# Layer norm rows moved from VectorE to ScalarE, with hand-written instruction orders rewritten in four places of each layer

## The chip, the cores and the metric

One Trainium2 chip, one core, no collectives. The metric is the device time in microseconds of one launch of the program (lower is better); every layer of every sequence runs inside that one launch.

## What is computed

Two sequences (BATCH = 2) of 1024 rows with 512 features go through two layers. A layer is attention followed by a small feed-forward product, each on a layer-normalised input and added to its input:

```python
x = x + attn(_layernorm(x), w_qkv, w_o)          # 32 heads of 16, 8 key/value heads, rope, causal softmax
x = x + scale * einsum(_layernorm(x), kernel*2-1) # kernel is 0/1, so the weights are -1/+1
```

`_layernorm` is `(x - mean) / sqrt(var + eps)` over the 512 features of a row, with no learned gain. The two layers differ in rope and in the layout of the weights. Everything is float32; the kernel keeps precision by splitting operands into a high and a low part and multiplying hi*hi + hi*lo + lo*hi.

## The kernel before, in words

A sequence is 8 tiles of 128 rows, kept in SBUF as `xs`. There are four rounds (2 sequences x 2 layers, `rounds`), written out one after the other, and each round has four stages. All five engines run their own program; nothing reorders it. The order on each engine is what the strings in the file say, and engines meet only through semaphores.

**Slots (first stage).** `SLOTS_A` counts slots n; `slot_work` turns a string of words into work, and `LAG` says for which tile t = n - lag a word works. In a slot TensorE turns one normalised tile (TX), multiplies the tile before by the qkv weights in four parts (Q.0 to Q.3), turns the head records of the tile two slots back in six quads (R.0 to R.5) into two PSUM banks, and computes row maxima products (U) of the tile three back. Behind Q stands a chain that crosses engines: ScalarE copies the projection (QC, `qkv_copy`), VectorE and GpSimd multiply by cos and sin (COS, `rope_sin`), VectorE adds (ROPE), ScalarE writes the high record parts (PH, `part_h`), GpSimd the low ones (`part_l`), and only then may R.0 of that tile start. The copies of R's quads are RC.1, 2, 4, 5 on ScalarE and RC.0, 3 on VectorE. The norm is made for a pair of tiles at a time: ST (`ln_stats`, VectorE), RS (`first_rstd`, ScalarE: Ln, then Exp), AP (`ln_a`, VectorE: four small Newton steps that refine 1/sqrt, and then two rows-times-scalar operations that write `xn`). HI and LO split a turned tile into its high part (ScalarE) and low part (VectorE).

**Groups 0 to 6.** For each of the 8 key/value heads, `GROUP_ORDER` interleaves on TensorE the softmax products S.p (two each, read by ScalarE's Exp at line 857), the value products PV, and the maxima products U.n of the *next* group, which VectorE reduces (`unit`, line 1027). The negated maxima are split by GpSimd (`nm_parts_of`), turned (N, `nm_turn`), copied to `nm_rows` by VectorE and sent by DMA (SP, line 463) to extra rows of `qT`, so that the product subtracts them. S.0 to S.4 need the maxima of chunk 0, S.5 and later those of chunk 1. X (`meet`) joins two halves of late maxima. The maxima of group 0 itself are made in the slots, those of the last tile (four units of 2 heads x 512 keys) after its last record copy and before S.0.

**Group 7 and the tail.** `LAST_ORDER` and `TAIL_ORDER` bring in, per tile, the turn and product of the output projection (CT, CP), its addition to `xs` (`add_wo`), the second norm (LS = `ln_stats`, LR = `first_rstd`, LM = `ln_newton`, LN = `ln_apply`, for tile pairs 0 to 3), the turn of the norm (DT, T), its split (H), the feed-forward product (DP) and its addition (`add_ffn`, line 1100). Pair 4 is pair 0 of the next round, and TA turns its first tile. WQ.c is ScalarE's split of a chunk of the next layer's qkv weights; GpSimd makes the low part of each chunk (line 1161, 128x768 with two SBUF inputs). DP of a tile waits for the addition of the tile two before it, since they share a PSUM bank.

In all orders an engine takes only its own words: of "T.4 DP.2 LM.3 WQ.0" TensorE takes T.4 and DP.2, VectorE the addition of DP.2 and then LM.3, ScalarE WQ.0.

## Time and profile before

| | us |
|---|---|
| device time, median of 3 runs | 1512.0 |
| the three runs | 1511.1, 1512.0, 1519.8 |
| the profiled execution's own time | 1511.48 |
| its span, first to last instruction | 1509.7 |
| TensorE busy | 1358.1 (90%) |
| VectorE busy | 1094.9 (73%) |
| ScalarE busy | 893.2 (59%) |
| GpSimd busy | 384.7 (25%) |

Times inside the trace are microseconds from the start of the span. A row of a timeline is: start, duration of the merged piece, engine, line, operation, output and input, how many instructions, and in brackets the idle time before it with what ended it.
### The profile page before, as it was taken

How to read it: one execution, taken by the hardware profiler on the slowest of the kernel's cores; microseconds unless marked ns; L12 is line 12 of the kernel's file. 1: busy time of each engine (PE TensorE's matmuls, PEld its weight loads, DVE VectorE, ACT ScalarE, POOL GpSimd, SP SyncE). 2: the span in 40 equal slices, each digit the busy share in tenths (PEclk: the TensorE clock that was granted, in tenths of full speed). 3: DMA queues.
4: the chain of work that ended last, by engine and by line, in shares of the span. 5: the costliest groups of instructions: out<-in, count | busy, mean ns of one | idle time of the engine just before them, and what ended most of it. 6: DMA issues, size and time to landing. Idle time of an engine off the chain costs nothing.

```text
span 1509.7 us, 28518 instructions
## 1 busy us (share of the span) xinstructions
PE 1358.1 (90%) x11076; PEld 796.5 (53%) x11076; DVE 1094.9 (73%) x1587; ACT 893.2 (59%) x1704; POOL 384.7 (25%) x591
## 2 busy tenths in 40 slices
PE   5989999999898999999889899999988889999997
PEld 4854444446675444444667544444567744444455
DVE  6667888847767888883776688888376668888647
ACT  3536776773354776775335377777624547777752
POOL 3422222111342222221134222222123412222201
PEclk9988999999897999999999699999999969999999
DMA  3000000001000000000220000000010000000011
GB/s 116 1 1 10 9 16 3 2 2 43 1 1 2 9 16 10 2 3 1 84 70 1 2 9 17 10 2 3 2 41 1 1 1 10 17 9 3 3 51 47
DMA packets 12980, 23.99 MB, mean 16 GB/s; under 512 B 1072, under 2 KB 4144, under 8 KB 12848
## 3 DMA queue, kind: packets, MB, share of 16 engines
q1 hardware_dynamic: 12848, 22.19, 4.3%
q8 instruction: 88, 1.44, 0.4%
q14 instruction: 44, 0.36, 0.1%
HBM read 16.94 MB, written 4.19 MB: 14 GB/s over the span
## 4 chain that ended last, share of the span: by engine, by line
PE 73%; DVE 16%; issue 6%; ACT 3%; POOL 1%; DMA 0%; DVEq 0%; ACTq 0%; POOLq 0%; SPq 0%
PE psO L675 20%; PE psM L539 15%; PE psE L654 14%; PE psM L612 12%; DVE mx L1027 8%; PE psE L592 3%; PE psO L592 3%; PE psM L522 2%; PE psM L619 2%; ACT probs L857 2%; DVE stats L934 1%; PE psM L639 1%; DVE xn L954 1%; DVE attn L1053 1%; PE psE L522 1%
## 5 line engine op out<-in xcount | busy, mean ns | idle before, releaser
L857 ACT ACTIVATE probs<-psE 128x512 f32<-128x512 f32 x1152 | 625.6, 596 | 293.4 <-PE psE L654 287.0
L1027 DVE TENSOR_REDUCE mx<-psM 128x2 f32<-128x768 f32 (+4 forms) x704 | 693.3, 1026 | 121.4 <-PE psM L619 96.3
L612 PE MATMUL psM<-kT,qT 48*128 48x384 f32 (+5 forms) x1536 | 314.5, 423 | 47.4 <-DVE mx L1027 36.6
L675 PE MATMUL psO<-probs,v_grp 128*32 128x512 f32 (+3 forms) x3072 | 324.3, 511 | 0.0
L654 PE MATMUL psE<-qT,kT 50*128 50x512 f32 (+3 forms) x1536 | 293.5, 420 | 15.3 <-ACT probs L857 10.2
L1227 POOL TENSOR_SCALAR_AFFINE_SELECT probs<-probs 128x512 f32<-128x512 f32 x256 | 160.0, 637 | 563.1 <-ACT probs L857 531.0
L612 PEld LDWEIGHTS psM<-kT,qT 48*128 48x128 f32 x1536 | 153.1, 196 | 161.6 <-DVE mx L1027 119.7
L654 PEld LDWEIGHTS psE<-qT,kT 50*128 50x128 f32 x1536 | 134.0, 191 | 171.6 <-ACT probs L857 127.2
L619 PE MATMUL psM<-mask_b 64*128 64x64 bf16 x2048 | 123.9, 201 | 0.0
L675 PEld LDWEIGHTS psO<-probs,v_grp 128*32 128x32 f32 x3072 | 68.4, 110 | 91.1 <-issue 68.5
L539 PE MATMUL psM<-wq_hi,xT_hi 128*128 128x512 f32 (+1 forms) x384 | 98.6, 379 | 9.2 <-ACT vs L823 4.7
L539 PE MATMUL psM<-w_lo,xT_hi 128*128 128x512 f32 (+1 forms) x384 | 96.2, 374 | 2.0 <-DVE w_lo L982 2.0
L539 PE MATMUL psM<-wq_hi,xT_lo 128*128 128x512 f32 (+1 forms) x384 | 93.3, 365 | 0.0
L619 PEld LDWEIGHTS psM<-mask_b 64*128 64x128 bf16 x2048 | 62.3, 100 | 57.6 <-issue 26.3
L809 ACT ACTIVATE xT_hi<-psM 128x512 fp32r<-128x512 f32 x64 | 37.7, 596 | 81.0 <-PE psM L522 66.5
L592 PE MATMUL psE<-ident,probs 128*128 128x128 f32 x384 | 66.8, 302 | 20.9 <-issue 15.0
L1174 POOL TENSOR_TENSOR attn<-attn,sin_s 128x320 f32<-128x320 f32 x64 | 64.5, 1028 | 50.5 <-ACT attn L822 50.0
L1183 POOL TENSOR_TENSOR probs<-attn,probs 128x512 fp32r<-128x512 f32 x32 | 41.9, 1308 | 137.7 <-ACT probs L834 137.7
L539 PEld LDWEIGHTS psM<-wq_hi,xT_hi 128*128 128x128 f32 x384 | 61.4, 190 | 22.3 <-issue 13.1
L539 PEld LDWEIGHTS psM<-w_lo,xT_hi 128*128 128x128 f32 x384 | 66.0, 195 | 12.8 <-DVE w_lo L982 2.7
L1001 DVE TENSOR_TENSOR attn<-attn,cos_s 128x640 f32<-128x640 f32 x32 | 32.2, 1005 | 54.8 <-ACT attn L822 54.0
L592 PEld LDWEIGHTS psE<-ident,probs 128*128 128x128 f32 x384 | 51.4, 155 | 36.6 <-issue 19.5
(80 smaller groups left out, 1304.0 us busy)
## 6 DMA issues: line engine op xcount, KB each, us to landing
probs<-in_w_qkv SPq DMA_DIRECT2D x5, 1536.0 KB, 6.5
xs<-in_x SPq DMA_DIRECT2D x8, 512.0 KB, 3.8
xn<-in_w_o SPq DMA_DIRECT2D x16, 256.0 KB, 2.5
out_x<-xs SPq DMA_DIRECT2D x8, 512.0 KB, 2.8
qT<-nm_rows SPq DMA_DIRECT2D x128, 8.0 KB
probs<-in_w_ffn SPq DMA_DIRECT2D x1, 256.0 KB, 8.3
attn<-in_mask SPq DMA_DIRECT2D x1, 160.0 KB, 7.8
sin_s<-in_sin SPq DMA_DIRECT2D x1, 128.0 KB, 8.0
```

Of the source, the lines that this page charges most:

```text
L522: ins = pe.transpose(dst[:, c * P:(c + 1) * P], src[:, c * P:(c + 1) * P], ident[:])
L539: ins = pe.matmul(dst, xT[:, k, c, :], w[:, c, n0:n1], start=first and i == 0, stop=last and i == len(some) - 1)
L592: ins = pe.transpose(bank[:, n * P:(n + 1) * P], src, ident[:])
L612: return pe.matmul(psM[:, 2 * pair + h % 2, to:to + k1 - k0], qT[lo:lo + MAXROW, g, qt // QT_PER_CHUNK, h // 2, qt % QT_PER_CHUNK * P:(qt ...
L619: return pe.matmul(psM[:, 2 * pair + h % 2, k0:k0 + P // 2], late_b[lo:lo + ROW, half, :], half_b[lo:lo + ROW, :], start=False, stop=half ...
L654: ins = pe.matmul(psE[:, (2 * p + a) % SRING, to:to + w], kT[lo:lo + DEPTH, g, kb * P:(kb + 1) * P], qT[lo:lo + DEPTH, g, c, j // 2, off:o ...
L675: ins = pe.matmul(psO[VW * j:VW * (j + 1), off:off + w], v_grp[:, kb, :], probs[:, (g * NS + s) % PSLOTS, at(j), to:to + w], start=s in (0 ...
L857: act.activation(probs[:, (g * NS + s) % PSLOTS, at(heads[0]):at(heads[0]) + len(heads), 0:w], psE[:, n % SRING, 0:w * len(heads)].rearran ...
L1027: dve.tensor_reduce(to, src, AX.X, ALU.max, negate=True).then_inc(ring_used.sem, 1)
L1174: ins = pool.tensor_tensor(t4[:, :, a, :], x4[:, :, 1 - a, :], sn[:, :, a * HALF:(a + 1) * HALF].to_broadcast([P, HEADS + KV, HALF]), ALU. ...
L1183: pool.tensor_tensor(q_parts[:, t % RECS, :, 2, :], rq, q_parts[:, t % RECS, :, 0, :].bitcast(F32), ALU.subtract)
L1227: ins = pool.affine_select(out=d, in_=d, compare_op=ALU.is_ge, fill=0.0, base=0, pattern=[[0, REP], [1, P]], channel_multiplier=-1)
```

## The change

Four things are changed; no matmul is added or removed.

1. **Norm.** ScalarE writes `xn` as mean - x (Identity, scale -1, bias from `mv`), with no rstd in it, right after the statistics. The Newton steps stay on VectorE (NW in slots, LM in the tail) with their sign turned, so that the two signs cancel. rstd is applied after the product: by ScalarE in the three copies of `qkv_copy`, as a per-row scale, and by VectorE in `add_ffn`, where the scalar is now rstd * scale. Statistics of a pair now wait until ScalarE has read those of two pairs before.
2. **First slots.** In slot 2 TensorE does the whole of Q of tile 2 before R of tile 0, and ScalarE's QC comes before RC. ST, RS and the norm stand in later slots (the next round's pair 1 is measured at the very end of the tail, LS.5).
3. **Last slots and group 0.** N of chunk 0 stands behind R.1 in the last slot. The last tile's four maxima units leave the slots and become V.0 to V.3 in `FIRST_ORDER`, an order of group 0's own; Y is their `meet`, and chunk 1's N and GpSimd's split of it come inside group 0.
4. **Group 7 and the tail.** New `LAST_ORDER` and `TAIL_ORDER`: DT.0 goes ahead of S.16, T.6 ahead of DP.4, T.7 ahead of DP.5, WQ.0 to WQ.3 earlier, and the norm's steps are spread anew.

```diff
@@ orders @@
+FIRST_ORDER = """
+V.0 S.0 V.1 S.1 V.2 S.2 V.3 Y S.3 U.0 PV.0.0 S.4 U.1 PV.1.0 N.1.0 U.2 PV.2.0 OC.0.0 U.3
+S.5 U.4 O.0.0 S.6 U.5 S.7 U.6 U.7 S.8 U.8 PV.3.0 S.9 U.9 U.10 S.10 PV.4.0 U.11 S.11 U.12 S.12 U.13 PV.5.0
...
-S.14 CP.2 LR.0 LM.0 LN.0 S.15 PV.6.0 CP.3 LS.1
-S.16 DT.0 S.17 PV.7.0 DT.1 LR.1 LM.1 LN.1 PV.8.0 PV.9.0
+S.14 CP.2 S.15 PV.6.0 DT.0 LR.0 S.16 CP.3 S.17 PV.7.0 DT.1 LS.1 LM.0 PV.8.0 PV.9.0
...
-CP.7 H.3 LS.3 LR.3 T.4 DP.2 LM.3 WQ.0 T.5 H.4 LN.3 WQ.1 DP.3 H.5 WQ.2 LS.4 DP.4 T.6 H.6 LR.4 WQ.3 DP.5
-LM.4 T.7 LN.4 H.7 DP.6 TA.0 DP.7
+DP.0 LN.1 LR.1 O.1.0 DP.1 LM.1 CT.4 CT.5 CP.4 CT.6 CP.5 CT.7 LS.2 T.2 CP.6 T.3 H.2 LN.2 LR.2 LM.2
+CP.7 H.3 LS.3 T.4 WQ.0 DP.2 WQ.1 H.4 T.5 LN.3 DP.3 LR.3 H.5 T.6 LS.4 WQ.2 DP.4 WQ.3 H.6 T.7 LN.4 LR.4 LM.3
+DP.5 H.7 DP.6 TA.0 LM.4 DP.7 LS.5
...
-       "RC": 2, "ST": -4, "RS": -3, "AP": -2}
-PE_SLOT = "TX U.0 Q.0 R.0 R.1 U.1 Q.1 R.2 U.2 R.3 Q.2 R.4 U.3 R.5 Q.3"
-ACT_SLOT = "HI RC.1 RC.2 RS PH RC.4 RC.5 QC"
-DVE_SLOT = "AP COS U.0 RC.0 LO ROPE U.1 RC.3 U.2 ST U.3"
-SLOTS_A = range(-4, TILES + 4)
-SLOT_NM = TILES + 1
+       "RC": 2, "ST": -3, "RS": -2, "NW": -1, "AP": -2}
+SLOT_FILL, SLOT_LAST = 2, TILES + 1
+PE_SLOT = {None: "TX U.0 Q.0 R.0 R.1 U.1 Q.1 R.2 U.2 R.3 Q.2 R.4 U.3 R.5 Q.3"}
+ACT_SLOT = {None: "HI AP RC.1 RC.2 RS PH RC.4 RC.5 QC"}
+DVE_SLOT = {None: "COS U.0 RC.0 LO ROPE U.1 RC.3 U.2 NW ST U.3"}
+PE_SLOT[SLOT_FILL] = "TX Q.0 Q.1 Q.2 Q.3 R.0 R.1 R.2 R.3 R.4 R.5"
+ACT_SLOT[SLOT_FILL] = "HI AP RS QC RC.1 RC.2 PH RC.4 RC.5"
+DVE_SLOT[SLOT_FILL] = "COS LO ROPE RC.0 RC.3 NW ST"
+PE_SLOT[SLOT_LAST] = "U.0 U.1 R.0 R.1 N U.2 R.2 R.3 U.3 R.4 R.5"
+DVE_SLOT[SLOT_LAST] = "U.0 U.1 RC.0 N U.2 RC.3 U.3"
+SLOTS_A = range(-4, TILES + 2)
@@ ScalarE @@
+            def ln_apply(q, i):
+
+                act.wait_ge(var_ready.sem, var_ready.after(q))
+                for k in range(2):
+                    act.activation(xn[:, k, :], tile_of(i % PAIRS, k), ACT.Identity, bias=mv[:, i % 2, k, 0:1],
+                                   scale=-1.0).then_inc(xn_ready.sem, 1)
...
+                def ln_d(i):
+
+                    if i == 0:
+                        act.wait_ge(ring_ready.sem, ring_ready.after(r * NJ + JOB["O", KV - 1, 0]))
+                    last = TILES - 1 if i == 0 else d_turn(2 * i - 1)
+                    act.wait_ge(turned.sem, turned.after(r * TURNS + last))
+                    ln_apply(r * (2 * PAIRS) + PAIRS + i, i)
...
                 def qkv_copy(t, k):
+                    if t % 2 == 0:
+                        act.wait_ge(lm_self.sem, lm_self.after((r * (2 * PAIRS) + t // 2) * LM_LINKS + 3))
                     act.wait_ge(projected.sem, projected.after(r * TURNS + t))
                     bank = qkv_bank(t)
-                    act.activation(qk[:, k, 0:DIM], psM[:, bank, :], ACT.Copy)
+                    by = rstd[:, t // 2, k:k + 1]
+                    act.activation(qk[:, k, 0:DIM], psM[:, bank, :], ACT.Copy, scale=by)
...
@@ VectorE @@
+                if q >= 2:
+                    wait_alone(dve, xn_ready.sem, xn_ready.after(q * 2 - 3))
+                    wait_alone(dve, rs_ready.sem, rs_ready.after(q - 2))
...
-                link(lm_self, q * LM_LINKS + 2, dve.tensor_scalar(newton[:], newton2[:], -0.5, 1.5, ALU.mult, ALU.add))
-                dve.tensor_tensor(rstd[:, i % 2], y, newton[:], ALU.mult).then_inc(lm_self.sem, 1)
-
-            def ln_apply(q, i):
-
-                wait_alone(dve, lm_self.sem, lm_self.after(q * LM_LINKS + 3))
-                for k in range(2):
-                    dve.tensor_scalar(xn[:, k, :], tile_of(i % PAIRS, k), mv[:, i % 2, k, 0:1], rstd[:, i % 2, k:k + 1],
-                                      ALU.subtract, ALU.mult).then_inc(xn_ready.sem, 1)
+                link(lm_self, q * LM_LINKS + 2, dve.tensor_scalar(newton[:, i % 2], newton2[:, i % 2], 0.5, 1.5, ALU.mult, ALU.subtract))
+                if to is None:
+                    dve.tensor_tensor(rstd[:, at], y, newton[:, i % 2], ALU.mult).then_inc(lm_self.sem, 1)
...
                 def add_ffn(t):
-                    dve.wait_ge(projected.sem, projected.after(r * TURNS + d_turn(t)))
-                    dve.scalar_tensor_tensor(out=xs[:, t, :], in0=psM[:, 2 + t % 2, :], scalar=scale_s[:, 0:1],
+                    if t % 2 == 0:
+                        dve.wait_ge(lm_self.sem, lm_self.after((r * (2 * PAIRS) + PAIRS + t // 2) * LM_LINKS + 3))
+                    wait_alone(dve, projected.sem, projected.after(r * TURNS + d_turn(t)))
+                    dve.scalar_tensor_tensor(out=xs[:, t, :], in0=psM[:, 2 + t % 2, :], scalar=rstd[:, PAIRS + t // 2, t % 2:t % 2 + 1],
                                              in1=xs[:, t, :], op0=ALU.mult, op1=ALU.add).then_inc(ffn_added.sem, 1)
...
@@ GpSimd @@
                         mask(g, s)
+                        if g == 0 and s == DIAGONAL[1]:
+                            nm_parts_of(0, 1)
...
                 nm_parts_of(0, 0)
-                nm_parts_of(0, 1)
                 group(0, True)
```

TensorE in slot 2 of a round: L522 (L546 after the change) turns a normalised tile, L539 (L563) is Q, L592 (L616) is R. Before:

```order
L522 MATMUL psE<-ident,xn 128x128 x4
L539 MATMUL psM<-wq_hi,xT_hi 128x512 x4
L592 MATMUL psE<-ident,probs 128x128 x4
L592 MATMUL psO<-ident,probs 128x128 x4
L539 MATMUL psM<-w_lo,xT_hi 128x512 x4
L592 MATMUL psE<-ident,probs 128x128 x4
```

The same slot after the change:

```order
L546 MATMUL psE<-ident,xn 128x128 x4
L563 MATMUL psM<-wq_hi,xT_hi 128x512 x4
L563 MATMUL psM<-w_lo,xT_hi 128x512 x4
L563 MATMUL psM<-wq_hi,xT_lo 128x512 x4
L563 MATMUL psM<-wq_hi,xT_hi 128x256 x4
L563 MATMUL psM<-w_lo,xT_hi 128x256 x4
L563 MATMUL psM<-wq_hi,xT_lo 128x256 x4
L616 MATMUL psE<-ident,probs 128x128 x4
L616 MATMUL psO<-ident,probs 128x128 x4
```

Six parts of Q stood around and behind the first R; now all of them stand ahead of it, and the six R follow one another.

TensorE from the last slots into group 0: L639 (L663) is N, L612 (L636) and L619 (L643) a maxima product and its mask, L654 (L678) an S. Before, from the end of the slot that has N behind it:

```order
L592 MATMUL psO<-ident,probs 128x128 x4
L639 MATMUL psE<-ident,nm_parts 128x128
L612 MATMUL psM<-kT,qT 128x448 x2
L592 MATMUL psE<-ident,probs 128x128 x4
```

```order
L592 MATMUL psO<-ident,probs 128x128 x4
L612 MATMUL psM<-kT,qT 128x512 x4
L619 MATMUL psM<-mask_b 128x64 x4
L612 MATMUL psM<-kT,qT 128x512 x4
L619 MATMUL psM<-mask_b 128x64 x4
L654 MATMUL psE<-qT,kT 128x512 x2
```

And after the change, the same two places:

```order
L616 MATMUL psO<-ident,probs 128x128 x4
L636 MATMUL psM<-kT,qT 128x448 x4
L643 MATMUL psM<-mask_b 128x64 x4
L616 MATMUL psE<-ident,probs 128x128 x4
L616 MATMUL psO<-ident,probs 128x128 x4
L663 MATMUL psE<-ident,nm_parts 128x128
```

```order
L616 MATMUL psO<-ident,probs 128x128 x4
L636 MATMUL psM<-kT,qT 128x512 x2
L678 MATMUL psE<-qT,kT 128x512 x2
L636 MATMUL psM<-kT,qT 128x512 x2
L643 MATMUL psM<-mask_b 128x64 x4
L678 MATMUL psE<-qT,kT 128x512 x2
L636 MATMUL psM<-kT,qT 128x512 x2
```

Two maxima products and two R now stand ahead of N, and an S stands between the last tile's maxima products.

VectorE in the tail: L973 (L1016) is the low part of a turned tile, L945 to L948 (L997 to L1003) the Newton steps, L954 the norm's rows, L1100 (L1147) the feed-forward addition, L934 to L939 the statistics. Before:

```order
L939 TENSOR_SCALAR var_eps<-mv 128x2
L1100 SCALAR_TENSOR_TENSOR xs<-psM,scale_s,xs 128x512
L945 TENSOR_TENSOR newton<-rs0 128x2
L946 TENSOR_TENSOR newton2<-newton,var_eps 128x2
L947 TENSOR_SCALAR newton<-newton2 128x2
L948 TENSOR_TENSOR rstd<-rs0,newton 128x2
L973 TENSOR_TENSOR xT_lo<-psM,xT_hi 128x512
L954 TENSOR_SCALAR xn<-xs,mv,rstd 128x512 x2
L1100 SCALAR_TENSOR_TENSOR xs<-psM,scale_s,xs 128x512
L973 TENSOR_TENSOR xT_lo<-psM,xT_hi 128x512
```

After, from the statistics of the same pair (pair 3) on:

```order
L991 TENSOR_SCALAR var_eps<-mv 128x2
L1147 SCALAR_TENSOR_TENSOR xs<-psM,rstd,xs 128x512
L1016 TENSOR_TENSOR xT_lo<-psM,xT_hi 128x512
L1147 SCALAR_TENSOR_TENSOR xs<-psM,rstd,xs 128x512
L1016 TENSOR_TENSOR xT_lo<-psM,xT_hi 128x512
L986 BN_STATS stats<-xs 128x6 x2
```

Between the first addition and the low part that the next product waits for, four Newton steps are gone; the rows of the norm are gone from this engine, and the Newton steps of the pair come two statistics later.

## Rows read from the trace of the kernel before

**Rows 1.** The page, busy time and granted clock in 40 slices.
```profile
PE 1358.1 (90%) x11076; PEld 796.5 (53%) x11076; DVE 1094.9 (73%) x1587; ACT 893.2 (59%) x1704; POOL 384.7 (25%) x591
...
PEclk9988999999897999999999699999999969999999
```

**Rows 2.** The waits: engine and line, releaser, us in total, times, longest.
```profile
PE psE L592 <- issue: 15.0, 4, 3.8
...
PE psM L539 <- DVE xT_lo L973: 12.7, 4, 4.5
...
PE psE L639 <- POOL nm_parts L1217: 9.6, 4, 2.4
...
PE psE L522 <- DVE xn L954: 18.9, 8, 9.5
```

**Rows 3.** Windows: us, then busy PE, PEld, DVE, ACT, POOL, then PEclk, DMA.
```profile
475.30:511.20 35.90, 32.37 (x278) 16.05 (x278) 28.38 (x33) 20.04 (x38) 6.08 (x13) 0.81 0.03 9
511.20:539.10 27.90, 26.33 (x272) 12.38 (x270) 23.56 (x29) 20.90 (x40) 7.33 (x14) 1.00 0.04 12
460.10:475.30 15.20, 11.88 (x81) 8.30 (x81) 11.32 (x15) 6.04 (x10) 4.47 (x6) 0.89 0.01 3
745.00:763.00 18.00, 11.66 (x50) 8.86 (x51) 16.21 (x25) 4.81 (x9) 8.29 (x6) 0.91 0.33 118
763.00:787.20 24.20, 20.17 (x121) 17.52 (x120) 15.96 (x38) 10.87 (x25) 8.30 (x9) 0.86 0.14 44
```

**Rows 4.** Timeline of TensorE in the second round's tail.
```profile
748.92 2.07 PE L539 MATMUL psM<-wf_s,xT_lo 128*128 128x512 f32 x4 [2.72 <-DVE xT_lo L973]
...
759.91 0.66 PE L522 MATMUL psE<-ident,xn 128*128 128x128 f32 x4 [2.88 <-DVE xn L954]
```

**Rows 5.** Timeline of VectorE in the same tail.
```profile
744.90 1.61 DVE L947 TENSOR_SCALAR newton<-newton 128x2 f32<-128x2 f32 x1
746.65 1.61 DVE L948 TENSOR_TENSOR rstd<-rs,newton 128x2 f32<-128x2 f32 x1
748.18 0.68 DVE L973 TENSOR_TENSOR xT_lo<-psM,xT_hi 128x512 fp32r<-128x512 f32 x1
```

**Rows 6.** Timeline of GpSimd in the same tail.
```profile
744.64 5.38 POOL L1161 TENSOR_TENSOR w_lo<-probs,wq_hi 128x768 fp32r<-128x768 f32 x3 [30.12 <-ACT wq_hi L802]
```

**Rows 7.** Groups by line and form: count, busy us, mean ns of one, idle before.
```profile
L954 DVE TENSOR_SCALAR xn<-xs,mv,rstd 128x512 f32<-128x512 f32 x66 | 39.0, 632 | 12.9 <-PE psE L522 8.8 <-DVE rstd L948 4.0
...
L809 ACT ACTIVATE xT_hi<-psM 128x512 fp32r<-128x512 f32 x64 | 37.7, 596 | 81.0 <-PE psM L522 66.5 <-PE psM L539 14.5
...
L792 ACT ACTIVATE ln_var<-mv,eps_s 128x2 f32<-128x2 f32 x33 | 9.7, 295 | 46.9 <-DVE mv L937 46.9
...
L794 ACT ACTIVATE rs<-ln_var 128x2 f32<-128x2 f32 x33 | 6.7, 203 | 1.0
```

**Rows 8.** Timeline of TensorE, first slots of the third round.
```profile
762.61 1.18 PE L539 MATMUL psM<-wq_hi,xT_hi 128*128 128x512 f32 x4
...
772.28 1.17 PE L539 MATMUL psM<-wq_hi,xT_hi 128*128 128x512 f32 x4
777.17 1.08 PE L592 MATMUL psE<-ident,probs 128*128 128x128 f32 x4 [3.72 <-issue]
...
785.69 0.60 PE L522 MATMUL psE<-ident,xn 128*128 128x128 f32 x4
```

**Rows 9.** Timelines of VectorE, ScalarE and GpSimd in the same slots.
```profile
770.36 0.83 DVE L1001 TENSOR_TENSOR attn<-attn,cos_s 128x640 f32<-128x640 f32 x1 [0.22 <-DVE var_eps L939]
...
772.61 1.06 ACT L833 ACTIVATE probs<-attn 128x1024 fp32r<-128x1024 f32 x1 [2.23 <-DVE attn L1009]
...
774.37 1.43 POOL L1183 TENSOR_TENSOR probs<-attn,probs 128x512 fp32r<-128x512 f32 x1 [4.54 <-ACT probs L834]
```

**Rows 10.** Timeline of TensorE, the second round's first S.
```profile
478.73 0.70 PE L654 MATMUL psE<-qT,kT 50*128 50x512 f32 x2
```

**Rows 11.** Timeline of SyncE's DMA issues after chunk 1's maxima copy.
```profile
484.26 1.26 SPq L463 DMA_DIRECT2D qT<-nm_rows  x2
```

124 lines of the change are left out of this document (69 added, 55 removed).

## The prediction

> **What bounds the kernel now.** I read the page first. TensorE is busy 90% of the span, no other engine over 73%, and its granted clock dips at the same places of all four rounds [rows 1]. So time can come only from TensorE's idle stretches and from the stretches at the lower of its two clock levels that follow them; nothing in the change shortens a matmul. Next the waits: one gap of 3.7 to 3.8 us before the record turns (L592), one of up to 4.5 us before the low products (L539), one of 2.4 us before the turn of the maxima (L639) occur four times each, once per round; the wait of the norm's turn for VectorE's rows (18.9 us in 8 places, of which 9.5 is the start of the program) is the fourth [rows 2]. Then windows around these places in one round of about 371 us [rows 3]. The steady groups are nearly full (TensorE 26.33 of 27.90 us at clock 1.00) and the change leaves groups 1 to 6 alone. What can be gained lies in four stretches, and I price each from there.
>
> **The tail.** In 745 to 763 TensorE is idle 18.00 - 11.66 = 6.3 us [rows 3]. The timeline shows why: the product of tile 4 waits 2.72 us for its low part, the turn of the next round's first tile 2.88 us for its rows [rows 4]. VectorE does that low part at 748.18, behind two Newton steps of 1.61 us each [rows 5]; the same four-step group has 128x2 operands and costs about 0.3 us a step elsewhere. GpSimd runs three 128x768 differences from 744.64, 5.38/3 = 1.8 us each [rows 6], and both steps end as one of these ends. So VectorE is both the bottleneck here (busy 16.2 of 18 us) and held up by GpSimd. 
> After the change: the two norm-row operations per pair leave VectorE (66 in all, mean 632 ns, [rows 7]: 1.3 us a pair), and Newton leaves the path from statistics to turn. The new path is statistics (2 x 0.64 + 0.5 us), then ScalarE's rows. ScalarE's copy of 128x512 takes 596 ns; the per-row operand costs what L792 (with one) has over L794 (without), 295 - 203 = 92 ns [rows 7], so 0.69 us a row tile. For pair 3 I follow the new orders: product of tile 7 ends 740.2, statistics to 743.1, rows by 744.4, and TensorE reaches T.6 at 744.9. No wait. The low part of tile 4 is then delayed only by var_eps waiting for GpSimd (up to 1.6 us): at 746.3 instead of 748.9, about 0.5 to 1 us of idle. DP.6 and DP.7 wait for additions two tiles back, another 1 us in all. So the next Q starts near 756 and not at 762.6. The 6.3 us idle plus about 1.2 us of halved clock (2.07 us for four matmuls that take 1.08 at full clock, [rows 4]) is 7.5; I keep 1.5 of it: gain 6.0 us, bounds 2 (another small VectorE step behind each of GpSimd's four) and 7.5.
>
> **First slots.** From the first Q at 762.61 to the turn that opens slot 3 at 785.69 are 23.1 us [rows 8]. Q with its turn takes (772.28 - 762.61)/2 = 4.8 us. The third Q is begun at 772.28 and its rest stands behind R.0, which waits 3.72 us and then runs with everything else at half clock: clock 0.86 over 24.2 us means 6.8 us at the lower level, some 2.5 us lost [rows 3, 8]. R.0's own chain is Q.3, QC, sin and cos, add, high part (1.6 us), low part (1.43 us and more) [rows 9]; cos began at 770.36 because statistics stood before it on VectorE. Those are gone from there; cos starts when QC ends, and R.0 is ready about 1.5 us sooner. The three pointer scales in QC put 0.28 us back. After: three Q back to back, 3 x 4.7 = 14.1 us, by when R.0 is ready (14.5 before, about 13.3 now). Then six R over two banks, each pair of R held by one copy of 0.6 to 0.7 us and its turn of 0.6: about 4.0 us where they were hidden before. Then PH of tile 1 stands behind RC.2 and R.0 of tile 1 comes 1 us late in slot 3. 14.1 + 4.0 + 1.0 = 19.1: gain 4.0. Bounds 0 (clock falls again in the sparse R stage, and lateness grows) and 6.2.
> The norm's ScalarE rows in slots 0, 2, 4 (1.3 us each) fill ScalarE's idle time: it is busy 10.87 of 24.2 us [rows 3]. I cost them at nothing; if the cover fails, 1.3 us three times a round.
>
> **Last slot.** N waits 2.4 us for GpSimd [rows 2]; the four matmul groups behind it run at half clock (0.89 over 15.2 us is 3.3 us at the lower level, some 1.5 us lost, [rows 3]). Now two maxima products (1.2 us) go first and R.0 waits for the same GpSimd work minus its last 0.6 us. 2.4 + 1.5 - 0.9 = 3.0 us. Bounds 1 and 4.
>
> **Group 0.** From the last tile's maxima to the next group's first S are 35.9 us, with VectorE busy 28.38 and TensorE 32.37 at clock 0.81 [rows 3]; before the first S at 478.73 [rows 10] TensorE waits three times for VectorE's maxima. All that VectorE work stays, in a single mixed stretch. A steady group has VectorE idle for 27.90 - 23.56 = 4.3 us. TensorE at full clock needs about the 26.3 us of a steady group. So VectorE sets the length: 28.4 + 4.3 = 32.7. A new wait: chunk 1's maxima go meet, GpSimd, N, copy, two DMA issues (1.26 us, [rows 11]), flight, S.5, with only U.2, PV.2 and U.3 between N and S.5. No row shows the flight; bounded by 0 and by the distance from issue to the S.5 that used it before, about 6 us. I take 2 us, near the 2.5 of the w_o loads, and then S.5 waits 1 to 2 us, half of it inside VectorE's 4.3. 35.9 - 32.7 = 3.2, less 0.4 more idle: about 3.0. Bounds -2 and 5.
>
> **Group 7** and the part of the tail before 745 have TensorE over 97% full, so T.6, T.7 and DT.0 earlier bring nothing beyond the tail term. At the start of the program the weights' low parts are the limit: 0.
>
> **Sum.** 6.0 + 4.0 + 3.0 + 3.0 = 16.0 us a round, 64 us in four. The profiled execution took 1511.5 (span 1509.7 and 1.8 around it), 0.5 under the median, which is nothing here. 1511.5 - 64 = 1447.5, on the median's scale 1448. The bounds add to 1 and 22.7 a round, that is 1508 and 1421; not all fall on one side together.
>
> **Rivals.**
> (a) Only the tail and the last slot pay; group 0 takes the rest back as VectorE's 28.4 us plus S.5's wait, and the R stage pulls the clock down. 6 + 3 = 9 less 1 a round: 36 - 4 = 32 us, 1480. For it: VectorE stands at 28.38 of 35.9 there already, and the R stage is sparse. Against: the low clock of that window (0.81) has idle time as its cause, and this is what goes.
> (b) All gaps close and no new one opens: near the upper bounds, 19.5 a round, 1434. Against: every new wait above.
> (c) The record chain becomes the period of the slots. PH(t+1) stands behind RC.2(t), which needs R.2(t); R.0(t+1) needs PH and the low parts. With tile 1 late from slot 2, the loop R.0, R.1, Q.1, R.2 (2.3 us), copy 0.7, PH 1.65, low parts 2.0 to 2.7, is 6.7 to 7.4 us against a slot of 8.2, so the lateness shrinks. It decides the run if rows of the norm on ScalarE and port waits bring the loop over 8.2 us; at 11.5 us (all of it doubled by such waits) six slots cost 6 x 3.3 = 20 us a round against 16 gained: 1511.5 + 16 = 1528.
> (d) By the Trainium skill, "TensorE: Matmul & The Clock Gate", sections on the clock gate, TensorE's clock is throttled by default and released by activity. The trace agrees: clock 1.00 in the full groups, 0.81 where it waits. It would bear out (a) if the six R alone are too little work, which no row of before shows, since they are never alone there.
>
> **Chances.** Forecast (1436 to 1462) 0.50; (a) 0.24; (b) 0.16; (c) and anything like it 0.10, of which half ends above 1497. A measurement here tells about 1% from no change. Faster by over 1% 0.93, within 1% 0.04, slower by over 1% 0.03. Range 1428 to 1484.
>
> **What would show it.** Right: Q to slot 3's turn 19 us and not 23; no 3.7 us gap before L616; the last DP at full clock with the next Q about 7 us sooner after the tail's start; the window of group 0 near 33 us with clock over 0.9; VectorE busy down by some 39 us, ScalarE up by 45 + 9. Wrong: gaps of TensorE before R in slots 3 to 8 (then c), a gap over 3 us before S.5, PEclk digits under 8 at the start of group 0 (then a), or ScalarE named as releaser of L563 after the change.

## The result, and the profile after

The changed kernel takes 1496.7 us, median of 17 runs that lie between 1483.5 and 1507.5, against 1512.2 before. The ratio is 0.9875, with a 95% interval of 0.9841 to 0.9909. That is 15.4 us, where 64 were forecast, and the time lies above the forecast range. Some executions of either kernel are over 1.5% longer than its fastest (the longest of before took 1574.6 us): medians here are of all runs, ratios leave such executions out.

First the page of the kernel after, to be read against [rows 1].

```profile
PE 1368.5 (91%) x11076; PEld 791.0 (53%) x11076; DVE 1041.6 (69%) x1526; ACT 942.4 (63%) x1770; POOL 383.9 (26%) x591
...
PEclk9999999999997899999999669989999998999999
```

VectorE lost 53 us and ScalarE gained 49 (39 and 54 were forecast), so the work went where the change sends it. The line of the clock is the surprise. The first round has lost its dip, the second and the fourth still have one, and in the third round, in the middle of the row, it has become two slices of 6 and, three slices on, an 8. TensorE executes the same 11,076 matmuls and is busy 10 us longer.

Next the profiled execution (1501.4 us, 4.7 over the median; span 1499.5, 10.2 less than before) is cut at five marks that both kernels have in each round: the last addition of w_o's output, ScalarE's copies of the values of the first and of the last row tile, the first exponential of group 1, and that of group 7. The forecast of each stretch is that of the prediction, times four.

| stretch, four rounds together | before, us | after, us | gained | forecast |
|---|---|---|---|---|
| tail: last w_o addition to the next first tile's copy (in the last round to the end) | 109.4 | 79.4 | 30.0 | 24 |
| slots: first tile's copy to the last tile's | 257.1 | 243.7 | 13.4 | 16 |
| last slot and group 0: last tile's copy to group 1 | 211.9 | 210.4 | 1.5 | 24 |
| groups 1 to 6 | 678.1 | 708.0 | -29.9 | 0 |
| group 7 and w_o's additions | 229.1 | 234.3 | -5.2 | 0 |

The first two stretches paid as forecast. The third paid almost nothing, and the six steady groups, whose instructions the change doesn't touch, became 30 us longer. Of these 30 us group 1 alone makes 16.6: it took 28.8, 31.4, 35.1 and 33.0 us in the four rounds, where before it took 27.9. The windows of the kernel after show how: group 0 (from its first exponential to that of group 1) in the four rounds, then groups 1 to 6 in the four rounds, then the tail of the second round, a steady group of the second round and one of the third (616.90 and 970.40), and 24 us within the third round's group 0. Columns are those of [rows 3].

```profile
98.40:134.30 35.90, 30.98 (x270) 15.25 (x270) 26.75 (x31) 20.17 (x38) 5.78 (x12) 0.81 0.04 9
460.00:498.90 38.90, 33.91 (x268) 16.06 (x266) 27.01 (x31) 20.14 (x38) 5.79 (x12) 0.74 0.03 9
830.20:874.00 43.80, 39.53 (x268) 18.17 (x266) 27.23 (x31) 20.17 (x38) 5.78 (x12) 0.62 0.02 8
1213.80:1249.20 35.40, 29.67 (x268) 14.54 (x266) 26.80 (x31) 20.14 (x37) 5.79 (x12) 0.87 0.04 9
...
134.30:306.00 171.70, 161.65 (x1594) 75.18 (x1596) 142.57 (x176) 124.75 (x233) 41.50 (x82) 0.98 0.02 7
498.90:674.60 175.70, 166.06 (x1598) 76.83 (x1598) 142.38 (x176) 124.87 (x232) 41.41 (x82) 0.95 0.03 7
874.00:1060.20 186.20, 177.23 (x1598) 81.35 (x1598) 142.58 (x176) 124.79 (x233) 41.45 (x82) 0.88 0.02 7
1249.20:1423.60 174.40, 164.97 (x1600) 76.61 (x1600) 142.35 (x176) 124.78 (x233) 41.49 (x82) 0.96 0.03 7
...
733.50:753.80 20.30, 19.19 (x102) 15.68 (x101) 16.33 (x38) 12.77 (x25) 8.75 (x6) 1.00 0.40 130
...
616.90:644.90 28.00, 26.42 (x270) 12.40 (x266) 23.58 (x30) 20.52 (x38) 6.09 (x13) 1.00 0.01 2
970.40:1001.20 30.80, 29.30 (x270) 13.42 (x266) 23.68 (x30) 20.93 (x39) 7.32 (x14) 0.89 0.01 3
...
843.30:867.60 24.30, 23.66 (x135) 10.60 (x135) 13.44 (x16) 11.10 (x21) 2.25 (x5) 0.51 0.03 12
```

Read the four windows of group 0 first. The number of instructions is the same but for two records, VectorE's and ScalarE's busy times are the same within 0.5 us, and the length follows the granted clock: 35.4 us at 0.87, 43.8 at 0.62. The steady groups do the same: 28.0 us at clock 1.00 and 30.8 at 0.89, with as many matmuls and nearly the same busy time on VectorE and ScalarE. In the third round five groups in a row stand at 0.89 or below. The last window is the plainest: TensorE is busy 23.66 of 24.30 us, waits for next to nothing, and has its lower level (1.2 GHz) nearly throughout (0.51).

The kernel before had groups at the lower level too. These are its groups 1 to 6 in the first two rounds:

```profile
141.80:310.90 169.10, 159.79 (x1596) 74.70 (x1597) 141.43 (x175) 124.78 (x232) 41.53 (x82) 0.99 0.03 7
511.10:681.80 170.70, 161.37 (x1596) 75.14 (x1598) 141.57 (x175) 124.78 (x233) 41.44 (x82) 0.98 0.02 7
```

Its worst round has 170.7 us at clock 0.98. In the profile after the change no round is that short.

Last come TensorE's waits after the change, to be read against [rows 2].

```profile
PE psE L678 <- ACT probs L908: 15.1, 34, 1.0
PE psE L616 <- DVE qT L1036: 10.1, 11, 2.2
PE psM L563 <- ACT vs L872: 9.6, 16, 1.1
PE psE L546 <- ACT xn L826: 7.8, 1, 7.8
...
PE psE L678 <- DMA qT<-nm_rows: 5.7, 4, 1.5
...
PE psM L546 <- DVE xT_lo L1016: 2.6, 4, 0.7
```

The waits of [rows 2] are gone or small: the 15.0 us ahead of the record turns, the 12.7 ahead of the tail's low products (2.6 now, ahead of a turn), the 9.6 of the turn of the maxima, and of the 18.9 us for the norm's rows only the start of the program is left (7.8). New is a wait of S.5 for the DMA of chunk 1's maxima (5.7 us). Others grew: Q for ScalarE's copy from 4.7 to 9.6, the record turns for VectorE's copies from 5.9 to 10.1, S for ScalarE's Exp from 10.2 to 15.1. So TensorE's idle time, span less busy time, fell from 151.6 to 131.0 us, that is by 20.6, and its busy time rose by 10.4: of more than 45 us of waits that went, over half came back as other idle time, half of the rest went into the same matmuls taking longer, and 10.2 us of span are left.

### The profile page after: what moved, and what is told of

Same layout as the page of the kernel before. It is cut to its first block, busy times and chain, and to the rows that moved or that the text cites. A ratio compares the mean times of both kernels' runs of the same rounds, so it can differ in the third digit from the quotient of the medians.

```text
span 1499.5 us, 28602 instructions
## 1 busy us (share of the span) xinstructions
PE 1368.5 (91%) x11076; PEld 791.0 (53%) x11076; DVE 1041.6 (69%) x1526; ACT 942.4 (63%) x1770; POOL 383.9 (26%) x591
## 4 chain that ended last, share of the span: by engine, by line
PE 70%; DVE 15%; issue 6%; ACT 6%; POOL 2%; DMA 1%; SPq 0%; DVEq 0%; ACTq 0%; POOLq 0%
PE psO L699 21%; PE psE L678 14%; PE psM L636 12%; PE psM L563 12%; DVE mx L1071 7%; PE psM L546 3%; PE psE L616 3%; PE psM L643 2%; PE psO L616 2%; ACT probs L908 2%; DVE stats L986 2%; POOL attn L1216 1%; PE psM L663 1%; DVE attn L1097 1%; DVE qT L1036 1%
## 5 line engine op out<-in xcount | busy, mean ns | idle before, releaser
L636 PE MATMUL psM<-kT,qT 48*128 48x384 f32 (+5 forms) x1536 | 319.3, 430 | 53.2 <-DVE mx L1071 35.0
L699 PE MATMUL psO<-probs,v_grp 128*32 128x512 f32 (+3 forms) x3072 | 348.3, 545 | 0.0
L678 PE MATMUL psE<-qT,kT 50*128 50x512 f32 (+3 forms) x1536 | 301.3, 431 | 25.3 <-ACT probs L908 15.1
L636 PEld LDWEIGHTS psM<-kT,qT 48*128 48x128 f32 x1536 | 157.3, 201 | 174.4 <-DVE mx L1071 115.7
L678 PEld LDWEIGHTS psE<-qT,kT 50*128 50x128 f32 x1536 | 138.2, 197 | 190.6 <-ACT probs L908 130.7
L643 PE MATMUL psM<-mask_b 64*128 64x64 bf16 x2048 | 125.5, 203 | 0.0
L563 PE MATMUL psM<-wq_hi,xT_hi 128*128 128x512 f32 (+1 forms) x384 | 98.6, 379 | 14.8 <-ACT vs L872 9.6
L563 PE MATMUL psM<-w_lo,xT_hi 128*128 128x512 f32 (+1 forms) x384 | 93.2, 365 | 2.0 <-DVE w_lo L1025 2.0
L643 PEld LDWEIGHTS psM<-mask_b 64*128 64x128 bf16 x2048 | 63.2, 102 | 59.7 <-issue 29.5
L563 PE MATMUL psM<-wq_hi,xT_lo 128*128 128x512 f32 (+1 forms) x384 | 92.6, 363 | 0.0
L563 PEld LDWEIGHTS psM<-wq_hi,xT_hi 128*128 128x128 f32 x384 | 61.8, 190 | 28.7 <-issue 19.0
L616 PE MATMUL psE<-ident,probs 128*128 128x128 f32 x384 | 60.7, 282 | 12.0 <-DVE qT L1036 10.1
L563 PEld LDWEIGHTS psM<-w_lo,xT_hi 128*128 128x128 f32 x384 | 64.3, 189 | 13.0 <-DVE w_lo L1025 2.7
L1016 DVE TENSOR_TENSOR xT_lo<-psM,xT_hi 128x512 fp32r<-128x512 f32 x64 | 43.6, 686 | 39.7 <-ACT xT_hi L842 39.1
L563 PEld LDWEIGHTS psM<-wq_hi,xT_lo 128*128 128x128 f32 x384 | 64.6, 190 | 10.0
```

The source lines that it names most:

```text
L563: ins = pe.matmul(dst, xT[:, k, c, :], w[:, c, n0:n1], start=first and i == 0, stop=last and i == len(some) - 1)
L616: ins = pe.transpose(bank[:, n * P:(n + 1) * P], src, ident[:])
L636: return pe.matmul(psM[:, 2 * pair + h % 2, to:to + k1 - k0], qT[lo:lo + MAXROW, g, qt // QT_PER_CHUNK, h // 2, qt % QT_PER_CHUNK * P:(qt ...
L643: return pe.matmul(psM[:, 2 * pair + h % 2, k0:k0 + P // 2], late_b[lo:lo + ROW, half, :], half_b[lo:lo + ROW, :], start=False, stop=half ...
L678: ins = pe.matmul(psE[:, (2 * p + a) % SRING, to:to + w], kT[lo:lo + DEPTH, g, kb * P:(kb + 1) * P], qT[lo:lo + DEPTH, g, c, j // 2, off:o ...
L699: ins = pe.matmul(psO[VW * j:VW * (j + 1), off:off + w], v_grp[:, kb, :], probs[:, (g * NS + s) % PSLOTS, at(j), to:to + w], start=s in (0 ...
```

## The experiments

Each ran beside the kernel before on the same chip. "After" is the changed kernel; where a kernel's edit is shown, words of the orders stand as in the change, and F is a new word, the filler: matmuls whose product goes into the output bank psO at a time when nobody reads it, and is overwritten by the next real product. Fillers add work and change no result.

**1. After, with group 0's order taken back.**

```
-SLOTS_A = range(-4, TILES + 2)
+SLOTS_A = range(-4, TILES + 3)
-    return words(GROUP_ORDER if has_prev else FIRST_ORDER)
+    return [w for w in words(GROUP_ORDER) if has_prev or len(w) < 3 or w[2] >= 0]
```

with the last tile's maxima back in the slots and the split of chunk 1's back in its old place.

> The changed kernel with group 0's own order taken back alone: the last tile's maxima stand in the slots again, and group 0 runs by the common order. Norm, first slots and tail stay as changed. Theory G (the new order of group 0 starves TensorE, so its clock falls there and in the groups behind it): groups 0 and 1 take again what they took before (31.9 and 27.9 us from first Exp to first Exp), the other gains stay, about 8 us a round in the tail and 7 in the slots: 1445 to 1460 us. Theory P (the clock falls by chance of phase in any group once things are shifted, whichever order stands in group 0): groups 1 to 6 show 29.5 to 31 us again in several places, 1475 to 1500 us.

Measured 1501.8 us (1480.5 to 1503.7, 10 runs), ratio 0.9881 [0.9836, 0.9926]. Neither number was met as a median. The profiled execution is one of the short ones, 1480.5:

```profile
106.80:138.30 31.50, 29.40 (x256) 14.57 (x257) 24.08 (x29) 19.95 (x38) 6.08 (x13) 0.80 0.04 11
470.40:502.40 32.00, 29.91 (x252) 14.42 (x248) 23.68 (x29) 19.92 (x37) 6.07 (x13) 0.78 0.03 10
836.20:868.30 32.10, 29.83 (x254) 14.81 (x254) 24.37 (x30) 19.93 (x38) 6.07 (x13) 0.79 0.04 10
1199.10:1230.60 31.50, 29.40 (x256) 14.59 (x258) 24.09 (x29) 19.97 (x38) 6.07 (x13) 0.80 0.04 10
...
502.40:677.40 175.00, 165.72 (x1598) 76.81 (x1598) 141.73 (x175) 124.88 (x233) 41.44 (x82) 0.95 0.03 7
868.30:1039.00 170.70, 161.39 (x1597) 75.29 (x1598) 141.62 (x175) 124.81 (x233) 41.48 (x82) 0.98 0.03 7
```

Group 0 is back at its 31.6 to 31.9 us of before, with the same low clock as before (0.8), and this execution took 21 us less than the profiled one of after. Yet seven of the ten runs lie at 1499.7 to 1503.7 us and three at 1480.5 to 1486.9, so over all runs taking the order back brought nothing (ratio 0.9881, after 0.9875). In this execution one round's steady groups (175.0) contain two long ones; what the longer runs look like was not recorded, but their distance of some 20 us would be seven groups of 30.8 in place of 28 (an estimate). So the order of group 0 isn't all of the loss: steady groups are also long in some runs and not in others of one program.

**2. Before, with group 0's new order alone** (the orders of slots, tail and group 7, and the norm's rows, as before).

```
-SLOTS_A = range(-4, TILES + 4)
+SLOTS_A = range(-4, TILES + 2)
+    return words(GROUP_ORDER if has_prev else FIRST_ORDER)
```

> The kernel before with group 0's own order alone added. Theory G: it loses what the changed kernel loses there, some 8 to 12 us a round less the 3 to 4 us that S gains by starting sooner: 1530 to 1550 us. Theory P: within 10 us of the kernel before, 1500 to 1520.

Measured 1561.0 us, ratio 1.0281 [1.0196, 1.0367]: some 43 us slower, for an order that the prediction priced at 12 us of gain.

```profile
106.80:146.40 39.60, 36.41 (x268) 17.44 (x266) 26.87 (x31) 20.10 (x38) 5.76 (x12) 0.66 0.03 8
487.60:530.70 43.10, 38.85 (x268) 17.86 (x266) 27.08 (x31) 20.13 (x38) 5.76 (x12) 0.62 0.03 8
...
912.20:1101.50 189.30, 180.22 (x1600) 82.42 (x1600) 142.75 (x176) 124.72 (x233) 41.32 (x82) 0.86 0.02 7
```

Group 0 is 39.6 and 43.1 us long at clock 0.66 and 0.62 in the first two rounds, and 35.3 and 35.4 at 0.87 and 0.86 in the others, where before it was 31.6 to 31.9. In the third round all of groups 1 to 6 follow at 30.7 to 35.3 us each (189.3 together). The new order of group 0 does this by itself in the kernel before. It is a strong result on the cause, but experiment 1 isn't its mirror: taking the same order out of the kernel after brought nothing over its ten runs. Why, stays open.

**3. After, with eight thin fillers in group 0** (two 50-row matmuls of 512 columns behind each of V.1, S.1, V.2 and V.3, to see whether a busy TensorE keeps its clock).

```
-V.0 S.0 V.1 S.1 V.2 S.2 V.3 Y S.3 U.0 PV.0.0
+V.0 S.0 V.1 F S.1 F V.2 F S.2 V.3 Y F S.3 U.0 PV.0.0
```

> The changed kernel with eight useless 512-column matmuls per round into the idle bank psO between the first S and V of group 0 (work added, none removed). If the low clock there comes of too little TensorE activity: the granted clock of group 0 rises from 0.62 to 0.87 in the profile of the changed kernel to over 0.9, and the time falls by 10 to 30 us although work is added. If VectorE or the waits set the length of group 0 and the clock is only a symptom: same time or up to 8 us more (2 us a round).

Measured 1490.6 us, ratio 0.9816 [0.9716, 0.9916], not to be told from after; but its windows say something. This is the second round; the others took 41.2, 44.2 and 39.1 us.

```profile
474.70:518.90 44.20, 42.16 (x278) 21.17 (x278) 27.03 (x31) 20.16 (x38) 5.79 (x12) 0.58 0.03 8
```

TensorE is busy 42.2 of 44.2 us, and its clock is 0.58, lower than in any group 0 of after. Idle time can't be what holds the clock down here. Nor does a low clock in group 0 always carry on: the groups 1 to 6 behind this one took 171.6 us, as few as in any round of after.

**4. After, with chunk 1's maxima turned earlier** (N.1.0 ahead of U.1, the split for it one diagonal sooner), against S.5's wait.

```
-S.4 U.1 PV.1.0 N.1.0 U.2 PV.2.0
+S.4 N.1.0 U.1 PV.1.0 U.2 PV.2.0
```

> The changed kernel with GpSimd's split and the turn of chunk 1's maxima one product sooner in group 0, so that their DMA lands before S.5 and the wait of 1.4 to 1.5 us there goes. If that gap is what brings the clock down for the rest of group 0: group 0 loses 4 to 8 us in each round, 1465 to 1480 us. If the sparse start alone does it: only the gap itself, 2 to 6 us in all.

Measured 1487.7 us, ratio 0.9778 [0.970, 0.9856]. The profiled execution is one of the long ones, 1509.9 us (four of six lie at 1480.8 to 1489.2). The wait for the DMA is gone from its trace, and group 0 of the third round still is 43.6 us long with a clock of 0.58:

```profile
835.20:878.80 43.60, 40.80 (x268) 18.77 (x266) 27.22 (x31) 20.18 (x38) 5.76 (x12) 0.58 0.02 8
```

So the low clock comes without the gap ahead of S.5 too. The interval of the ratio overlaps that of after, so whether the 1.4 us a round are won is open, and of the shorter executions there is no trace.

**5. After, once more** (nothing is edited).

> The changed kernel itself once more, for a second profile of the same instructions. Theory L (a group's length follows the granted clock, and which groups are hit changes from run to run with nothing in the program): groups 1 to 6 take one of the same few lengths (27.9, 29.5, 30.8 us), in other places than in the first profile, and group 0's length stays on the line through the first profile's four values (35.4 us at clock 0.87 to 43.8 us at 0.62). Rival W (each group's length is fixed by the order and its waits): every group repeats its length to 0.3 us.

1496.0 us. Group 0 took 39.0, 38.9, 42.7 and 38.9 us, where the first profile had 35.9, 38.9, 43.8 and 35.4:

```profile
99.90:138.90 39.00, 34.04 (x268) 15.89 (x266) 26.85 (x31) 20.14 (x37) 5.79 (x12) 0.74 0.03 9
...
829.70:872.40 42.70, 38.28 (x268) 17.69 (x266) 27.23 (x31) 20.15 (x38) 5.79 (x12) 0.64 0.02 8
```

One program and one order, and a length that in the main goes with the clock granted (38.9 us stood at 0.74 in one profile and at 0.69 in the other). Groups 1 to 6 took 171.6, 171.7, 179.5 and 170.0 us, 692.8 together against 708.0 in the first profile and 678.1 before. So a single profile's distribution over the rounds means little, and nor does the exact share of the steady groups in the loss; that group 0 is long is stable.

**6. After, with twelve full-array fillers in group 0** (the places of experiment 3, three matmuls of 128 rows each, on a weight that lies in SBUF).

```
+elif what == "F":
+    pe.wait_ge(o_copied.sem, o_copied.after((r * KV + g) * CHUNKS - 1))
+    for c in range(3):
+        pe.matmul(psO[:], wf_s[:, c, 0:P], wf_s[:, c, :], start=True, stop=True)
```

> As the run with useless matmuls at the start of group 0, but each of them now uses all 128 rows and 128 columns of the array (12 of 512 columns a round, some 3 us at full clock). If what the clock answers to is how much of the array works: group 0's clock rises above 0.9 and it takes 31 to 35 us instead of 35 to 44; 1460 to 1480 us. If a busy TensorE at half clock is simply what group 0 gives: clock stays 0.6 to 0.8 and it takes longer by the work added, 1495 to 1520 us.

Measured 1488.9 us, ratio 0.9836 [0.9764, 0.9908].

```profile
100.20:136.40 36.20, 31.65 (x280) 15.65 (x278) 26.80 (x31) 20.12 (x38) 5.76 (x12) 0.91 0.03 9
```

Now all four rounds read 36.2 to 36.3 us, at clock 0.91: the 39 and 44 us are gone, and no steady group takes 30 us or more. Full-array fillers do what thin ones didn't, though there were twelve of them and not eight. But the stretch is still long. From the last tile's first maxima product on, as the forecast counts, it takes 37.1 us, and the forecast was 32.7; the twelve fillers make some 3 us of that (an estimate: four matmuls of this size start within 1.02 us at full clock). Neither VectorE (26.8 of 36.2 us busy) nor TensorE (31.7) is full. How much of the rest is the order and how much the clock of 0.91, no run separates.

**7. After, with fillers in each of groups 1 to 6** (four full-array matmuls where TensorE waits 0.67 and 0.24 us for VectorE), against the long steady groups.

```
-S.0 U.0 U.1 PV.8.-1 S.1 U.2 PV.9.-1 N.1.0 S.2 OC.1.-1 U.3 U.4 U.5
-S.3 U.6 S.4 PV.0.0 U.7
+S.0 U.0 U.1 PV.8.-1 S.1 U.2 PV.9.-1 N.1.0 S.2 OC.1.-1 U.3 U.4 F U.5
+S.3 F U.6 S.4 PV.0.0 U.7
```

> The changed kernel with four useless full-array matmuls in each of groups 1 to 6, in the two places where TensorE waits 0.67 and 0.24 us for VectorE. If these waits are what lets the clock fall in groups of 29.5 and 30.8 us: all groups 1 to 6 take 27.9 to 28.8 us, and the time falls by 10 to 30 us though work is added. If not: each group is 0.2 to 0.9 us longer and the 30.8 us groups remain, 1500 to 1515 us.

Measured 1519.6 us, the median of eight runs from 1495.9 to 1553.1; ratio 0.9935 [0.9864, 1.0007]. That these waits bring the clock down is refuted: each group became 1.05 us longer (29.0 in place of 27.9), and groups of 30.5 and 32.0 us remained beside them. The same shows in experiment 8, which has these fillers too (29.0, 30.5 and, once, 33.8 us).

**8. After, with another order for group 0 and fillers everywhere.** The last tile's maxima go first and in one piece, then group 0 follows the common order, and fillers stand at its start and in groups 1 to 7. The split of chunk 1's maxima is back ahead of group 0, as before the change, here and in experiments 9 to 11.

```
-V.0 S.0 V.1 S.1 V.2 S.2 V.3 Y S.3 U.0 PV.0.0 S.4 U.1 PV.1.0 N.1.0 U.2 PV.2.0 OC.0.0 U.3
+V.0 F V.1 F V.2 F V.3 F Y S.0 F U.0 U.1 F S.1 U.2 N.1.0 S.2 F U.3 U.4 F U.5
+S.3 F U.6 S.4 PV.0.0 U.7
+...
```

> The changed kernel with an order of group 0 that makes the last tile's maxima first and then follows the common order, and with useless full-array matmuls wherever TensorE waits: between the last tile's maxima, at the start of every group 0, in groups 1 to 6 and at the start of group 7. If array activity holds the clock: group 0 near 31 us from first Exp to first Exp minus nothing for the clock, no 30.8 us groups, 1430 to 1455 us, the fastest of all. If activity added so does nothing: as the run that takes group 0's order back (1480 to 1502 us) plus 10 us of added work.

Measured 1500.6 us, ratio 0.9916 [0.9889, 0.9942]. The sum hides two opposite results.

```profile
103.10:131.90 28.80, 27.67 (x266) 13.36 (x267) 23.25 (x29) 19.96 (x38) 6.07 (x13) 1.00 0.04 12
674.50:697.30 22.80, 20.22 (x121) 9.06 (x117) 3.06 (x8) 13.83 (x26) 3.83 (x8) 0.85 0.01 3
```

Group 0 has clock 1.00 in all four rounds and takes 28.8 us, fillers included. Since the last tile's maxima now stand ahead of its first exponential, this isn't to be held against the 36 us of the change's order: from the last tile's first maxima product to group 1 it is 33.9 us, where before it was 35.7 to 36.5 and in experiment 6 37.1. But fillers in groups 1 to 6 cost their 1.05 us each, and in group 7 (second row, to the first w_o addition) up to 22.8 us stand against 17.9 to 19.3 before.

**9. As 8, with fillers at the start of group 0 alone.** There are nine F of two matmuls, 18 a round (the text on record says 16).

```
-S.0 U.0 U.1 PV.8.-1 S.1 U.2 PV.9.-1 N.1.0 S.2 OC.1.-1 U.3 U.4 F U.5
-S.3 F U.6 S.4 PV.0.0 U.7
+S.0 U.0 U.1 PV.8.-1 S.1 U.2 PV.9.-1 N.1.0 S.2 OC.1.-1 U.3 U.4 U.5
+S.3 U.6 S.4 PV.0.0 U.7
...
```

> The changed kernel with the last tile's maxima first, group 0 then by the common order, and 16 useless full-array matmuls a round in its first stretch only (the ones in groups 1 to 7 of the run with fillers everywhere are left out). If the clock is what the new order of group 0 lost: group 0 takes 28 to 29 us at clock 1.00 in all four rounds, groups 1 to 6 go back from 29.0 to 27.9 (or 29.5) us, 1450 to 1470 us, faster than the kernel before and the changed one. If the gain of the fillers is taken back in later groups: 1480 to 1500 us.

Measured 1454.1 us (1450.9 to 1461.5, 6 runs), ratio 0.9600 [0.9563, 0.9637]. It is faster than before and than after, beyond doubt: its longest run is 22 us below the shortest of after.

Its line of the clock on the page, then group 0 and groups 1 to 6 of its first two rounds in windows:

```profile
PEclk9999999999999999999999999999999999999999
```

```profile
103.60:132.40 28.80, 27.67 (x264) 13.34 (x264) 23.19 (x29) 19.93 (x37) 6.07 (x13) 1.00 0.04 12
461.50:490.30 28.80, 27.67 (x264) 13.33 (x264) 23.20 (x29) 19.93 (x37) 6.08 (x13) 1.00 0.04 12
...
132.40:303.10 170.70, 161.33 (x1598) 75.22 (x1598) 141.55 (x175) 124.77 (x232) 41.52 (x82) 0.98 0.03 7
490.30:665.20 174.90, 165.57 (x1598) 76.77 (x1598) 141.64 (x175) 124.88 (x232) 41.44 (x82) 0.95 0.02 7
```

For the first time no slice of the page is under 9. Groups 1 to 6 are 170.7 us in three rounds and 174.9 in one. Of the 24 steady groups two take over 30 us (the first two of the second round), where after had eight and its second profile four. That most long groups of after followed from what stood in front of them fits this, but is argued from single profiles. Cut at the marks of the first table, this execution (1461.5 us) gained 30.0 us in the tail, 13.5 in the slots and 21.6 in the last slot and group 0, and lost 8.9 in groups 1 to 6 and 5.3 behind them.

**10. As 9, with thin fillers**: the same number, columns and places, but 48 rows of keys and queries in place of 128.

```
-pe.matmul(psO[:], wf_s[:, c, 0:P], wf_s[:, c, :], start=True, stop=True)
+pe.matmul(psO[:], kT[0:MAXROW, g, 0:P], qT[0:MAXROW, g, 0, 0, :], start=True, stop=True)
```

> The run before this one with the same number of useless matmuls of the same 512 columns in the same places, but of 48 rows of the array instead of 128. If rows in work are what holds the clock: group 0 stays at clock 0.6 to 0.8 and 31 to 44 us, as without them or worse. If any busy TensorE holds it: as the full-array fillers, group 0 at 28 to 29 us.

**11. As 9, without any filler.**

```
-V.0 F V.1 F V.2 F V.3 F Y S.0 F U.0 U.1 F S.1 U.2 N.1.0 S.2 F U.3 U.4 F U.5
-S.3 F U.6 S.4 PV.0.0 U.7
+V.0 V.1 V.2 V.3 Y S.0 U.0 U.1 S.1 U.2 N.1.0 S.2 U.3 U.4 U.5
+S.3 U.6 S.4 PV.0.0 U.7
```

> The same order without any useless matmul, the control for the two. Clock theory: group 0 at clock near 0.8 and 31 to 32 us as in the run that takes group 0's order back, in all 3 to 6 us a round slower than with full-array fillers. If instead the order (maxima first) brought the 28.8 us of group 0 and not the fillers: it is as fast or faster, with clock 1.00.

Experiment 10 measured 1497.0 us, ratio 0.9855 [0.9779, 0.9931], and experiment 11 measured 1484.2 us, ratio 0.9785 [0.9726, 0.9843]. Neither is near 1454. Windows of 10: its first group 0, the start of its third, and the third round's groups 1 to 6. Then windows of 11: its first group 0, and groups 1 to 6 of its last round.

```profile
106.90:140.60 33.70, 32.74 (x262) 18.15 (x261) 23.55 (x29) 19.92 (x37) 6.05 (x13) 0.77 0.04 10
...
832.40:843.00 10.60, 10.60 (x72) 8.62 (x71) 7.44 (x9) 4.05 (x8) 1.31 (x4) 0.50 0.01 2
...
866.80:1051.30 184.50, 175.38 (x1598) 80.22 (x1598) 141.88 (x175) 124.74 (x232) 41.32 (x82) 0.89 0.02 7
```

```profile
103.40:135.90 32.50, 30.40 (x254) 14.74 (x252) 23.77 (x29) 19.97 (x38) 6.07 (x13) 0.76 0.04 10
...
1245.60:1430.10 184.50, 175.37 (x1596) 80.23 (x1598) 141.95 (x175) 124.77 (x233) 41.48 (x82) 0.89 0.02 7
```

Together with 9 this is the cleanest comparison of the study: the same order three times. With thin fillers TensorE is busy 10.60 of 10.60 us at the start of group 0 and has the lower level all the while. Without fillers it is idle there more, and group 0 reads 0.76 to 0.78, with thin ones 0.75 to 0.79. With full-array fillers it reads 1.00. At this place the clock was held when matmuls that use all 128 rows were added, and not by a busy engine alone. The two kinds of filler differ in one more thing, the numbers that they multiply (weights of the feed-forward product, keys and queries); no run tells rows from values. The last row of each block shows what can follow: without full-array fillers the six steady groups of a round stand at 0.89 and take 184.5 us. Of 11 the profiled execution, 1509.4 us, is the longest of four (the others took 1476.1 to 1490.7), so such rounds are rarer there than its trace says.

**12. Before, with the same nine pairs of full-array fillers**: four behind the last tile's maxima products, five in the first third of group 0. This tells whether the 1454 is the fillers' work alone.

```
+def fill():
+    pe.wait_ge(o_copied.sem, o_copied.after((r * KV) * CHUNKS - 1))
+    for c in range(2):
+        pe.matmul(psO[:], wf_s[:, c, 0:P], wf_s[:, c, :], start=True, stop=True)
...
+if g == 0 and (what, *arg) in (("S", 0), ("U", 1), ("S", 1), ("S", 2), ("U", 5)):
+    fill()
```

> The kernel before, with the same nine pairs of filler matmuls per round (128x128 by 512 columns, into the output bank, whose value is overwritten) that gave 1454: four behind the last tile's maxima products and five in the first third of group 0. Nothing else is changed. Theory C (the change's gains are real and only its clock was lost; fillers and change bring different things): the fillers here win back the clock of group 0 (31.6 us at 0.78 before; 28 to 30 us at 0.95 and over now) and cost 18 x 0.22 = 4 us, so that the kernel is 1500 to 1515 and stays well above 1454. Rival F (the 1454 is the fillers' work alone, the change brings nothing): the kernel before reaches 1450 to 1475 with them. Between these (1475 to 1500) part of the gain of 1454 is the fillers' own, and the change's part is what is left.

Measured 1514.5 us, ratio 0.9992 [0.9972, 1.0012]. Seven of its twelve runs lie at 1508.5 to 1518.5 us, five at 1543.8 to 1569.5.

```profile
111.50:139.70 28.20, 26.91 (x260) 12.88 (x257) 23.07 (x27) 19.95 (x38) 6.07 (x13) 1.00 0.04 12
481.40:509.60 28.20, 26.90 (x262) 12.86 (x256) 23.03 (x27) 19.93 (x37) 6.07 (x13) 1.00 0.04 11
...
829.50:852.10 22.60, 18.89 (x117) 12.27 (x117) 16.96 (x20) 6.30 (x12) 4.46 (x6) 0.85 0.01 2
```

Theory C holds. Group 0 falls from 31.9 to 28.2 us at clock 1.00, but the last slot in front of it becomes 1.1 us longer (the last window above) and more groups are of the 29.5 us kind (eight, five before), so next to nothing is left. With fillers in both, the kernel with the change's tail, slots and last slot stands at 1454.1 and the one without at 1514.5 (1509.3 is the median of its seven shorter runs): 55 to 60 us apart. That this is near the 64 of the forecast is in part luck, since the order of group 0 in experiment 9 is not the change's.

The profiles side by side, one execution each, cut at the marks of the first table:

| profile | last slot and group 0, four rounds, us | groups 1 to 6, us | of the 24 groups, over 30 us |
|---|---|---|---|
| before | 211.9 | 678.1 | 0 |
| after | 210.4 | 708.0 | 8 |
| 5, after again | 215.9 | 692.8 | 4 |
| 6, full-array fillers in the change's order | 203.4 | 686.1 | 0 |
| 9, maxima first, full-array fillers | 190.3 | 687.0 | 2 |
| 10, maxima first, thin fillers | 213.1 | 694.7 | 6 |
| 11, maxima first, no filler | 200.8 | 719.2 | 17 |
| 12, before with full-array fillers | 201.9 | 682.6 | 0 |

## Why the prediction was wrong

**The tail: right, and somewhat better.** 6.0 us a round were forecast, bounds 2 and 7.5; 7.3 to 8.2 were gained, about and over the upper bound. The clock of the tail, 0.91 in [rows 3], is 1.00 after. The norm's row takes 723 ns on ScalarE against the 0.69 us worked out from the pointer operand's 92 ns; the copy of Q's product takes 685 ns against 596 + 92. The collision with GpSimd came elsewhere than forecast: var_eps of pair 3, which was to wait for it, takes 0.26 us (at 736.54), and a Newton step takes 1.14 us at 743.81 and ends as GpSimd's MEMSET does (743.69 + 1.23). The product two tiles on then waits 0.46 us for the addition behind that step. This agrees with the Trainium skill, "SBUF — State Buffer", section on the two separate sides, as the prediction used it: of two operations that share the ports the second waits out the first. That the Newton step was in the two-port mode no trace shows.

**The first slots: right.** Forecast 4.0 us, from 23.1 to 19.1 between a layer's first Q and the turn that opens slot 3. In the third round, which [rows 8] shows, it is 20.4 us after (748.42 to 768.82), in the second and fourth 18.9, in the first 23.4 in place of 27.3: gains of 2.7 to 4.3. Over all slots 2.7 to 4.1 us a round were gained. Q's waits for ScalarE (9.6 us in all, 4.7 before) are the pointer scales' price and stayed small. Rival (c) did not come.

**The last slot: right.** Forecast 3.0, bounds 1 and 4. The last tile's first maxima product starts 13.0 us after its value copy, in the third round 14.0, where before it was 17.0, and 15.7 in the second round: 2.6 to 4.0 gained.

**Group 0: wrong, and this is the step that failed.** The prediction said "TensorE at full clock needs about the 26.3 us of a steady group. So VectorE sets the length: 28.4 + 4.3 = 32.7". TensorE did not have full clock. From the last tile's first maxima product to group 1 the four rounds took 36.7, 39.7, 44.6 and 36.2 us, where before it was 35.7 to 36.5. The forecast was 32.7. In rounds one and four it is about its length of before, in the others 4 and 8 us longer, at clock 0.74 and 0.62 within group 0. I had taken the low clock of [rows 3] (0.81) for a consequence of idle time, and so expected it to go with the idle time. Experiments 3 and 10 show that it stays when the idle time is filled with 48 or 50-row matmuls, and 6 and 9 that it goes, in part or wholly, when 128-row ones stand there. The change puts the maxima of the last tile (48 rows) next to the scores of group 0 (50 rows); that this mixture is what lowers the clock is my reading, and no run isolates it. S.5's new wait was forecast at 1 to 2 us and measured at 1.4 to 1.5; experiment 4 has the low clock without it.

**"leaves groups 1 to 6 alone": wrong, and a sum of the same size.** No instruction of theirs moved, and they cost 29.9 us more, 14.7 in the second profile (experiment 5). Groups 2 to 6 take 28.0, 29.5 or 30.8 us by the clock they find, group 1 up to 35.1, and the low clock can carry on for five groups, in experiment 10 for six. The prediction put this term at nothing. Of the gap between forecast and measurement in the profiled execution (64 - 10.2 = 54 us), groups 1 to 6 make 30, last slot and group 0 22.5, group 7 and w_o's additions 5, slots 3, and the tail gives back 6. For group 7 the prediction said that TensorE is over 97% full there; in its first 19.3 us of the second round before it was busy 16.74. That stretch took 17.9 us in three rounds and 19.3 in one, and after the change 17.9 in one and 19.4 in three, again with the clock (0.91).

**The rivals.** (a) had 0.24 and came nearest, with its sign "PEclk digits under 8 at the start of group 0". Its 1480 was still too low, since it too held group 0 at its length of before and the steady groups at theirs. For (d) the full groups at clock 1.00 agree with the rule from the Trainium skill, "TensorE: Matmul & The Clock Gate", section on the clock gate, that activity releases the clock. What I made of it was that a busy engine counts as active, and the 10.60 of 10.60 us at 0.50 in experiment 10 contradict that. No case of mine had the order of group 0 costing by itself what it does in experiment 2 (43 us in all); the bound of -2 a round for it was set from VectorE's side alone.

**What stays open.** Whether the rows of a filler or the values in it hold the clock was not told apart, why 48 and 50-row matmuls don't hold it was not measured outside this kernel, and fewer full-array ones than 18 a round were not tried in this order. Why a steady group falls to 0.89, and why in some runs it does so five times in a row and in others not at all, isn't settled; experiment 7 only speaks against its inner waits. And of the tail, what ScalarE's norm rows bring without the new orders was not tried.

## What to carry to other kernels

When an edit takes idle time from the busiest engine, check in the windows what that engine runs in the stretch and at which clock: the price of a stretch on TensorE depends on its instructions and on the clock, and here stretches at half clock took back most of the gain, a good part of it in groups that nobody had touched. Where such a stretch must stand, a few full-array matmuls into a bank that is free can pay (18 a round brought some 28 us by the ratios of experiments 9 and 11; in the kernel before they brought nothing, experiment 12), but in full groups they are plain cost (0.26 us each, experiment 7). And if the length of a program's stretches comes in steps from run to run, compare medians of many runs and read two profiles before explaining one.

## What the runs showed of the hardware that was not expected

- TensorE kept its lower level for nearly all of 24.3 us (0.51) while it was busy 23.66 of them almost only with matmuls that use part of the array (48, 50 or 64 rows, or 32 outputs; after, 843.30 to 867.60). With nine pairs of matmuls of 128 rows and 128 outputs around the start of group 0 it kept the higher one for all 28.8 us (experiment 9).
- The same instructions got different clocks at different places of one program: steady groups took 28.0 us and 30.8 us (after, 616.90 and 970.40), the products of probabilities and values in them 1.07 and 1.94 us for eight matmuls.
- A DMA of the 32x128 maxima within SBUF: the copy ends at 840.73, SyncE issues two transfers until 842.03, and the matmul that waits for them starts at 843.34. So copy to use is 2.6 us, of which the flight after the last issue is 1.3.

```profile
840.45 0.28 DVE L1084 CAST nm_rows<-psM 32x128 fp32r<-32x128 f32 x1 [1.04 <-PE psM L663]
```

```profile
840.76 1.27 SPq L486 DMA_DIRECT2D qT<-nm_rows  x2
```

```profile
843.34 0.50 PE L678 MATMUL psE<-qT,kT 50*128 50x512 f32 x2 [1.48 <-DMA qT<-nm_rows]
```
